# Second layer of a two-layer graph network: LayerNorm's gain folded into the weights, and a group's scattered products summed in one PSUM bank before they are added

## The reference

```
h = concat(x[src], x[dst], edge_attr) @ W1 + b1                  # one row per edge
h = relu((h - mean(h)) * rsqrt(var(h) + 1e-5) * ln_g + ln_b)     # LayerNorm with gain and bias
messages = (h @ W2 + b2) * sigmoid(edge_attr @ gate_w + gate_b)
agg = segment_sum(messages, dst)                                 # sum of an edge's row into its node
gi, gh = agg @ W_ih.T + b_ih, x @ W_hh.T + b_hh                  # then a GRU step per node
x = layernorm(x + gru(gi, gh, x))
```

## Time and profile before

| what | us |
|---|---|
| device time, three runs | 5134.09, 5176.93, 5184.84 |
| median of these | 5176.93 |
| span of the profiled execution, first to last instruction | 5142.6 |
| of it: sort and schedule | to about 472 |
| first layer | to about 2640 |
| second layer | to 5142.6 |

### The profile page before, as it was taken

One profiled execution on the slowest core, in us unless ns is written; L12 is line 12 of the kernel. 1 busy time (PEld: TensorE's weight loads), 2 busy tenths in 40 slices (PEclk: granted clock), 3 DMA queues, 4 the chain that ended last, 5 costly groups with the idle time before them and its releaser, 6 DMA issues. The chain is left out here.

```text
span 5142.6 us, 108062 instructions
## 1 busy us (share of the span) xinstructions
PE 3506.5 (68%) x20734; PEld 3121.8 (61%) x20735; DVE 4015.9 (78%) x15806; ACT 2380.6 (46%) x6569; POOL 3316.3 (64%) x3375
## 2 busy tenths in 40 slices
PE   5543666666666666666547877777777777777776
PEld 4432555656665565655547767666666666666665
DVE  8995677777777777777758988877877877877876
ACT  2211233333333333333336665665665655665654
POOL 0004777777777777777747777666666666666661
PEclk9655677776767777678868898888889888898887
DMA  3113445555555554555444444333333333333331
GB/s 105 45 35 92 130 139 145 145 142 145 145 142 144 146 145 142 143 144 145 142 107 106 108 110 105 97 96 98 94 96 100 96 92 100 95 95 100 98 94 40
DMA packets 597657, 576.83 MB, mean 112 GB/s; under 512 B 320530, under 2 KB 462744, under 8 KB 597312
## 3 DMA queue, kind: packets, MB, share of 16 engines
q0 software_dynamic: 133952, 329.07, 23.6%
q1 hardware_dynamic: 463360, 244.62, 17.8%
HBM read 536.53 MB, written 43.09 MB: 113 GB/s over the span
## 5 line engine op out<-in xcount | busy, mean ns | idle before, releaser
L1662 POOL DMA_INDIRECT crows<-c,gather_index x1664 | 1666.9, 1002 | 738.8 <-issue 469.7
L1187 POOL DMA_INDIRECT bxrows<-bx,gather_index x1664 | 1620.0, 974 | 507.5 <-issue 506.0
L1222 PE MATMUL scattered<-bxrows,hotw 128*128 128x129 f32 x3328 | 695.2, 378 | 552.7 <-DVE hotw L1385 552.0
L1222 PEld LDWEIGHTS scattered<-bxrows,hotw 128*128 128x128 f32 x3328 | 604.7, 272 | 634.5 <-DVE acc L1382 553.9
L1710 PE MATMUL scattered<-z,hotw 128*128 128x129 f32 x3328 | 560.1, 336 | 503.3 <-DVE hotw L1912 503.2
L1710 PEld LDWEIGHTS scattered<-z,hotw 128*128 128x128 f32 x3328 | 518.3, 242 | 534.8 <-issue 489.5
L1891 DVE SCALAR_TENSOR_TENSOR z<-h,rstd,ln_g 128x128 f32<-128x128 f32 x1664 | 577.6, 347 | 237.8 <-issue 237.5
L1212 PE MATMUL pre<-near,hotT 128*128 x3328 | 595.1, 352 | 211.2 <-DVE h L1360 177.8
L1695 PE MATMUL pre<-w1e,efT 128*128 128x129 f32 x3328 | 691.6, 291 | 66.8 <-DVE h L1883 34.0
L1382 DVE TENSOR_TENSOR acc<-acc,scattered 128x129 f32 x1664 | 471.2, 283 | 326.2 <-ACT mask L1293 320.6
L1212 PEld LDWEIGHTS pre<-near,hotT 128*128 128x128 f32 x3328 | 558.1, 260 | 261.2 <-issue 257.9
(11 more groups left out here) (268 smaller groups left out, 5599.5 us busy)
## 6 DMA issues: line engine op xcount, KB each, us to landing
spread<-place_rows SPq DMA_DIRECT2D x416, 256.0 KB, 3.5
ef<-in_edge_attr SPq DMA_DIRECT2D x1664, 32.0 KB
bxrows<-bx,gather_index POOLq DMA_INDIRECT x1664
crows<-c,gather_index POOLq DMA_INDIRECT x1664
x_turned<-x1T SPq DMA_DIRECT2D x98, 64.0 KB
g_xT<-x_turned SPq DMA_DIRECT2D x98, 64.0 KB
x_a<-in_x SPq DMA_DIRECT2D x97, 64.0 KB
x_b<-in_x SPq DMA_DIRECT2D x97, 64.0 KB
```

The costliest lines, as they stand in the source:

```text
L1187: pool.indirect_dma_start(out=bx[q][:, k, 0:2 * D], out_offset=None, in_=s.bx[:, :], in_offset=bass.IndirectOffsetOnAxis(ap=s.index[:, g * ...
L1222: last = nc.tensor.matmul(out[:, k // 2, k % 2, 0:W], hotw[v % 2][:, k, :], bx[v][:, k, D:D + W], start=True, stop=True)
L1662: pool.indirect_dma_start(out=crows[q][:, k, 0:D], out_offset=None, in_=s.c[:, :], in_offset=bass.IndirectOffsetOnAxis(ap=s.index[:, g * G ...
```

## The change

1. **ln_g is folded into the weights.** `centre` multiplies W1's columns with the sign of ln_g, `copy_folded` multiplies the rows of the folded GRU weights with its size (at least 1e-30). Since relu(a·size + b) = size·max(a, -b/size) + b, line 1891 can now take the maximum with -ln_b/size (`floor_b`) itself, as its second operation, in place of the multiplication with ln_g. The separate maximum (line 1907, two instructions a group) and its semaphore `scaled` go. Four small dependent instructions at the head of the second layer make `floor_b`.
2. **From group 37 on (`FIRST_JOINED`) a group's products are summed on PE.** The sorting by rounds leaves a group of eight steps with at most three different tiles from there on. PE clears three places of one bank with a matmul of zeros (`nothing`), and then lets all eight products accumulate, each at the place of its tile: the tile of step 0 at place 0, the tile of step 7 at place 2, any other at place 1. The place is a register value, from a new table `spot_of`, which `schedule_stage` makes and PE loads as eight registers for each group. DVE adds three sums in place of eight products, after all eight z rather than between them. Groups 0 to 36 still add eight.
3. **Loops.** `joined_slots` stands in the place of `loop_slots`: rounds 4 to 9 are written out, the loop with node work has rounds 10 to 51, and its bodies are of the joined kind. POOL's program is as before.

```diff
         for j in range(2):
-            dve.tensor_scalar(s.w1cd[:, j * D:(j + 1) * D], raw[:, j, :], mean[:, j:j + 1], None, ALU.subtract)
+            dve.scalar_tensor_tensor(s.w1cd[:, j * D:(j + 1) * D], raw[:, j, :], mean[:, j:j + 1], sign_g[:, :],
+                                     ALU.subtract, ALU.mult)
...
-        dve.tensor_copy(fold[:, :], m_ps[:, :, :].rearrange("p j d -> p (j d)")).then_inc(rows_done, 1)
+        dve.tensor_scalar(fold[:, :], m_ps[:, :, :].rearrange("p j d -> p (j d)"), size_g[:, 0:1], None,
+                          ALU.mult).then_inc(rows_done, 1)
...
+                        dve.tensor_copy(tile_rows[own, :], tile_turned).then_inc(spotted, 1)
...
+                        dve.scalar_tensor_tensor(spot_i[own, :], same_last[own, :], 1.0, same_first[own, :],
+                                                 ALU.add, ALU.mult).then_inc(spotted, 1)
...
+JOINED = 10
+FIRST_JOINED = JOINED * R - 3
+LEADS = (0, 3, 7)
+def joined_slots(engine, steps, nodes, last):
+    def body(o):
+        for q in range(R):
+            steps(o * R + q, q, o, o >= JOINED)
+            nodes(o * R + q, q, o)
+    body(0)
+    with engine.Fori(1, 4) as o:
+        for q in range(R):
+            steps(o * R + q, q, o, False)
+    for o in range(4, JOINED):
+        body(o)
+    with engine.Fori(JOINED, BODIES) as o:
+        for q in range(R):
+            steps(o * R + q, q, o, True)
+            nodes(o * R + q, q, o)
...
+def sums_added(n):
+    if isinstance(n, int) and n <= FIRST_JOINED:
+        return n * G + 1
+    return n * 3 + (FIRST_JOINED * (G - 3) + 1)
...
+                sp.dma_start(spot_of, s.spot_of[:, :]).then_inc(steps_in, 16)
...
-                    if has(g, 3):
+                    if has(g, 3) and joined:
+                        par = (q - 3) % 2
+                        spots = load_values(nc, mybir.EngineType.PE, spot_of[0:1, bass.ds((g - 3) * G, G)], 2 * W)
+                        pe.wait_ge(added, sums_added(g - 3))
+                        nc.tensor.matmul(out[:, 0, 0:3 * W], nothing[:, 0:P], nothing[:, :], start=True, stop=False)
+                        for k in range(G):
+                            if k % 4 == 0:
+                                pe.wait_ge(hotw_made, g * 2 - 5 + k // 4)
+                                pe.wait_ge(z_made, g * 2 - 5 + k // 4)
+                            last = nc.tensor.matmul(out[:, 0, bass.ds(spots[k], W)], hotw[par][:, k, :],
+                                                    z[par][:, k, :], start=False, stop=(k == G - 1))
+                        last.then_inc(scattered, 1)
+                    elif has(g, 3):
...
-                                                            rstd[:, par, k:k + 1], ln_g[:, :], ALU.mult, ALU.mult)
+                                                            rstd[:, par, k:k + 1], floor_b[:, :], ALU.mult, ALU.max)
                             if k % 4 == 3:
-                                last.then_inc(scaled, 1)
-                        if has(g, 3):
+                                last.then_inc(z_made, 1)
+                        if has(g, 3) and not joined:
...
-                        if has(g, 2) and k % 4 == 3:
-                            half = k // 4
-                            dve.wait_ge(scaled, g * 2 + half - 3)
-                            part = z[par][:, 4 * half:4 * half + 4, 0:D]
-                            dve.tensor_tensor(part, part, spread_b, ALU.max).then_inc(z_made, 1)
+                    if has(g, 3) and joined:
+                        dve.wait_ge(scattered, g + (FIRST_JOINED * 2 - 2))
+                        for j, k in enumerate(LEADS):
+                            dve.wait_ge(added, sums_added(g - 3) + j)
+                            place = acc[:, bass.ds(tiles[k], 1), 0:W]
+                            dve.tensor_tensor(place, place, out[:, 0:1, j * W:(j + 1) * W], ALU.add).then_inc(added, 1)
```

More of the change, by code:

```diff
@@ L751, in schedule_stage @@
         side_rows = one("side_rows", [P, BLOCKS, P], I32)
-        edge_i, chunk_x = one("edge_i", [BLOCKS, P], I16), one("chunk_x", [P, BLOCKS], F32)
+        edge_i, chunk_x = one("edge_i", [BLOCKS, P], I16), one("chunk_x", [P, 32 + BLOCKS], F32)
+        own = slice(32, 32 + BLOCKS)
+        tile_rows, same_first, same_last, spot_i = (
+            one(n, [32 + BLOCKS, P], t) for n, t in (("tile_rows", F32), ("same_first", F32), ("same_last", F32),
+                                                     ("spot_i", I16)))
         tile_sq, ones_sq = one("tile_sq", [P, P], BF16), one("ones_sq", [TILES, TILES], F32)
@@ L787, in _ @@
                 sp.dma_start(s.edge_of.rearrange("a (b p) -> (a b) p", p=P), edge_i[:, :]).then_inc(stored[1], 16)
+                sp.wait_ge(spotted, 4)
+                sp.dma_start(s.spot_of.rearrange("a (b p) -> (a b) p", p=P), spot_i[own, :]).then_inc(stored[1], 16)
                 for l in LAYERS:
@@ L936, in _ @@
                     if l == 1:
-                        dve.tensor_tensor(chunk_x[:, :], chunk_f[l][:, :], by_block[l][:, :, 2],
-                                          ALU.add).then_inc(chunk_copied, 1)
+                        dve.tensor_tensor(chunk_x[:, 0:BLOCKS], chunk_f[l][:, :], by_block[l][:, :, 2], ALU.add)
+                        dve.tensor_copy(chunk_x[:, own], by_block[l][:, :, 0]).then_inc(chunk_copied, 1)
                 for l in LAYERS:
@@ L1478 @@
 BEHIND = 4
+JOINED = 10
+FIRST_JOINED = JOINED * R - 3
+LEADS = (0, 3, 7)
+assert FIRST_JOINED * G // TILES >= 3
+def joined_slots(engine, steps, nodes, last):
[13 more added lines that the diff above has]
+            nodes(o * R + q, q, o)
+    for g in range(GROUPS, last + 1):
+        steps(g, g % R, g // R, True)
+        nodes(g, g % R, g // R)
+def sums_added(n):
+    if isinstance(n, int) and n <= FIRST_JOINED:
+        return n * G + 1
+    return n * 3 + (FIRST_JOINED * (G - 3) + 1)
 THIRDS = [(0, 3), (3, 6), (6, G)]
@@ L1489, in layer1_stage @@
         sem = s.sem
-        step_rows = sb("step_rows1", [2, STEPS], I16)
-        tile_of, edge_of = step_rows[0:1, :], step_rows[1:2, :]
+        step_rows = sb("step_rows1", [3, STEPS], I16)
+        tile_of, edge_of, spot_of = step_rows[0:1, :], step_rows[1:2, :], step_rows[2:3, :]
+        nothing = sb("nothing", [1, 3 * W], BF16)
         spread = [sb(f"spread1_{q}", [P, G * P], BF16) for q in range(2)]
@@ L1673, in _, with steps @@
                 pe.wait_ge(aug_ready, 1)
-                def steps(g, q, o):
+                def steps(g, q, o, joined):
                     if has(g, 0):
@@ L1746, in nodes @@
                         last.then_inc(n_made, 1)
-                loop_slots(pe, steps, nodes, LAST)
+                joined_slots(pe, steps, nodes, LAST)
             @block.scalar
@@ L1857, in _ @@
                 dve.memset(eps[:, :], 1e-5)
+                dve.memset(nothing[:, :], 0.0)
                 dve.memset(augT[:, :], 1.0).then_inc(aug_ready, 1)
@@ L2001, in program @@
         s.tile_order = [nc.dram_tensor(f"tile_order{l}", (1, TILES), I16).ap() for l in range(2)]
-        s.edge_of = nc.dram_tensor("edge_of", (1, STEPS), I16).ap()
+        s.edge_of, s.spot_of = (nc.dram_tensor(n, (1, STEPS), I16).ap() for n in ("edge_of", "spot_of"))
         s.index1, s.place1 = (nc.dram_tensor(n, (P, STEPS), t).ap() for n, t in (("index1", I32), ("place1", F32)))
```

98 lines of the change are left out of this document (64 added, 34 removed).

## The result

The changed kernel takes 4856.88 us (median of 4 runs, 4849.13 to 4887.46) against 5178.77 us (4 runs, 5134.09 to 5184.84): a ratio of **0.943, 95% interval 0.937 to 0.949**. The profiled execution has a span of 4854.2 us and a time of 4857.32; the span of before was 5142.6, so the trace to be explained is 288.4 us shorter. The prediction had said 279 for that difference and 4898 us for the median.

A forecast was written before the change was run, and what follows sets the result against it. The prediction took DVE to bound the kernel after group 36. -276 us for 171 groups, +1 at the start and -4 at the end gave -279, from 5176.9 to 4898 us; whole range 4845 to 4975.

The forecast's parts named there:

- POOL becomes the bound: Second layer after group 36: POOL's 32 gathers a round, 41.4 us, outlast DVE's round of 36.9 us; forecast chance 0.73.
- The top of a round, 4.5 us: DVE's issue idle time before first h and z, 3.60 and 2.45 us, loses 4.5 us a round; other bound 0.
- z and adds, 1.55 us a slot: DVE from first z to first hotw: 4.94 us falls to 3.4, saving 1.55 a slot, 6.2 a round.
- DVE's round of 36.9 us: DVE's loop round: 47.57 less 6.2 for z and adds and 4.5 at the top; 41.4 if the top stays.
- the rival in which DVE stays the bound: Top keeps its 4.5 us and adds cost their upper bound: 43.8 us a round, 4998 us; chance 0.17.
- The sum, -276 for 171 groups: Groups 36 to 207 at 8 gathers of 1.295 us take 1771.6 us instead of 2047.9, h following POOL at 12.2 us.
- PE's second load at nothing, zeros 0.4 to 0.7 us: PE's added register load, 1.93 us a slot, hidden; zeros matmul 0.4 to 0.7 us; PE's round 38.3, below 41.4.
- the two PE rivals: PE's register loads exposed: new one alone 46.0 us a round, 5096 us, chance 0.06; both 53.7, 5425 us, 0.03.
- The wait for the whole group, covered by 1.3 us: DVE's first add waits for all eight products; 5.8 us of DVE work ahead covers at most 3.80 + 0.7.
- Groups 0 to 36 at nothing, the start at +1: Groups 0 to 36 lose their maxima but POOL sets their pace: nothing; small extra instructions in `centre` cost about 1 us.
- The end, -4 us: After h of group 207, 62.0 us: cheaper z and adds and fewer last adds save 4 us (0 to 5.5).
- The median, 4898: Whole-kernel time: median 5176.9, 34 us above the profiled span, less 279; own range 4874 to 4925.

The follow-up runs named there:

- half of the gathers: Every second gather of layer 2 left out, part of the sums missing: changed kernel 4599.59 us, ratio 0.893; kernel before 5150.46 us, ratio 0.999.
- both shift runs: The kernel before with 64 or 256 one-column memsets on DVE ahead of layer 2's loops, loop untouched: ratios 0.960 and 1.002.
- the folding alone: The changed kernel with folded weights but no group joined, eight adds one by one, no zeros, no second register load: 4850.36 us, ratio 0.943.
- the joining alone: The changed kernel with joined products but ln_g not folded, so two maxima a slot return on DVE: 4890.22 us, ratio 0.952.
- the kernel moved by 64: The kernel before with 64 memsets on DVE ahead of layer 2's loops, so its loop starts 64 instructions later: 4934.95 us, ratio 0.960.
- the one moved by 256: Control: the kernel before with 256 memsets on DVE ahead of layer 2's loops: 5154.34 us, ratio 1.002.
- the 16 matmuls: 16 extra matmuls on PE, results overwritten, ahead of the first layer's products: changed kernel 4847.07 us, folding alone 4841.94 us, kernel before 5140.51 us.
- the folding with half of the gathers: The folding alone with every second gather of layer 2 left out, part of the sums missing: 4715.87 us.
- the gate on ACT: The changed kernel with the gate computed on ACT by logarithm and exponential instead of DVE's add and reciprocal: 4892.49 us, ratio 0.945.

## Why the prediction was right, step by step

- **POOL becomes the bound:** shown. With half of the gathers the 171 groups of the changed kernel gain 210 us and those of the kernel before 9.
- **The top of a round, 4.5 us:** right in size (2.45 us went to 1.01; ahead of the first h DVE now waits for gathers, and with half of them out the 3.60 are 0.28), and for the reason given: where the loop lies decides, as both shift runs show. The count that the prediction leaned on, 217 instructions being fewer than the 262 that don't stall, isn't what decides: 273 don't stall in the folding alone, and 289 don't when they lie 64 places further on. By the Trainium skill's rule ("Runtime: NRT & Kernel Launch", instruction fetch mechanics) the other bound, 0, was never live for this body, since 217 instructions can't touch three blocks of 256.
- **z and adds, 1.55 us a slot:** measured 1.77 (4.94 to 3.17). The folding brings the larger part: in the folding alone the phase of the last group takes 3.78 us (z at 4790.33, hotw at 4794.11 in its trace). The joining is worth 1.9 us a round once POOL is out of the way. With POOL as the bound neither size of the joining's share is seen in the time; without the joining the kernel is as fast.
- **DVE's round of 36.9 us:** at most 36.2, the round with POOL out of the way, so the rival in which DVE stays the bound (41.4 to 43.8) falls.
- **The sum, -276 for 171 groups:** measured -287.9. The term that was off is the gather's pitch: from the first gather of group 36 (3019.02 us) to that of group 207 (4776.65) it is 1.285 us instead of 1.295, inside the bounds of 1.280 and 1.310. The other term, h at 12.2 us behind its group's first gather, is 11.3 at group 36 and 13.7 at group 207, which gives 2.4 us back. The prediction had feared that gathers get longer when all engines work more densely; they got shorter, 981 ns instead of 1002 in the mean. The maxima aren't the cause, since the joining alone has them and 981 ns too; the kernel moved by 64 has 986, the one moved by 256 has 1005. What it is in the stalled loop that lengthens them stays open.
- **PE's second load at nothing, zeros 0.4 to 0.7 us:** the zeros take 0.33 to 0.53 us, 0.33 as a rule. The load of places is hidden even at a round of 36.2 us, and that round lies below the 46.0 and 53.7 of the two PE rivals, so both fall. The prediction's reason, that a load runs while the engine works off what was issued, holds for this load and not for the load of tile numbers: with half of the gathers out that one leaves PE idle for some 2 us a round. While POOL sets the pace this isn't seen in the time.
- **The wait for the whole group, covered by 1.3 us:** right in the loop, where the adds of the round above start without a gap. At the end, where DVE has neither h nor z of a next group ahead of the add, it isn't covered: the last group's adds wait 2.15 us for PE's products.
- **Groups 0 to 36 at nothing, the start at +1:** -2.3 us up to h of group 36. The reason, that POOL sets the pace there, was right by a margin of 5 us only (half of the gathers left out of the kernel before).
- **The end, -4 us:** off by 6 us in the profiled execution, where the span after the last h grew by 1.9, and right in another, of the same code (below). The saving came: the last group's adds end 21.0 us behind the last h (4811.3) instead of 26.3 (5106.8). PE's node products behind them gave it back. First PE's timeline of before there, then the same products after:

```profile
5102.98 0.70 PE L1731 MATMUL bank_gru<-wfold_sb,g_T 128*128 128x256 f32 x2 [0.82 <-ACT augT L1822]
5103.52 0.59 PE L1732 MATMUL bank_gru<-whh_sb,g_xT 128*128 128x256 f32 x2
```

```profile
4811.68 1.22 PE L1812 MATMUL bank_gru<-wfold_sb,g_T 128*128 128x256 f32 x2 [0.82 <-ACT augT L1903]
4812.69 1.06 PE L1813 MATMUL bank_gru<-whh_sb,g_xT 128*128 128x256 f32 x2
```

  And the granted clock (the number behind the five busy times), before from 5103 to 5108 us and after from 4811 to 4819:

```profile
5103.00:5108.00 5.00, 3.42 (x12) 1.92 (x12) 2.92 (x10) 1.44 (x2) 0.00 (x0) 1.00 0.07 18
```

```profile
4811.00:4819.00 8.00, 6.38 (x12) 3.35 (x12) 0.88 (x3) 1.44 (x3) 0.00 (x0) 0.50 0.06 16
```

  Before, PE had 2.4 GHz for these twelve matmuls, after it had 1.2 GHz, as it had from 4796 us on. But this comes and goes in the changed kernel. With the 16 matmuls ahead of the first layer its end is the same code; there the granted clock is 0.99 from 4804 to 4811 us, and the same products are as short as before:

```profile
4806.00 0.70 PE L1819 MATMUL bank_gru<-wfold_sb,g_T 128*128 128x256 f32 x2 [0.82 <-ACT augT L1910]
4806.54 0.59 PE L1820 MATMUL bank_gru<-whh_sb,g_xT 128*128 128x256 f32 x2
```

  58.0 us follow its last h, 4.1 less than the 62.0 of the kernel before, which is what was forecast. Of the five traces of the changed kernel and its variants with joined groups and folded weights, three have 63.3 to 63.9 us after the last h and two 58.0 and 58.2; the five of the kernel before and its variants all have 61.8 to 62.1. The folding alone has a granted clock of 0.97 from 4806 to 4812 us and needs 59.2. Some 13 to 16 us ahead of these products PE had waited in all three kernels: 4.75 us for DVE's hotw in the kernel before, 3.85 us for DVE's adds in the changed kernel, and 5.88 us with the 16 matmuls. What decides whether the clock comes back is open.
- **The median, 4898:** 41 us too high, and the forecast's own range (4874 to 4925) missed it; the whole range held. The sum was taken off a median that lay 34 us above the profiled span, and the median after lies 3 us above its span. The step that failed is the assumption that this offset belongs to the kernel and stays: it comes and goes from one execution to the next.

## What to carry to other kernels

An "issue" gap of some us at a loop's top that another loop with the same work lacks is worth one cheap test before anything is rewritten: move the loop by a few dozen instructions, and by a whole block as a control. When an edit makes the next engine the bound, half of that engine's work left out tells what the edit's parts are worth, which the time itself no longer does. When an added instruction changes nothing, count it in the trace first: it may not be there. And a median should be set against the profiled span by the stage that differs, not carried over as an offset.

## What had not been expected of the hardware

The 36 us between runs sit in one place: PE's products ahead of the first layer. The busy times of that stretch in the changed kernel, and in the changed kernel with the gate on ACT, where the stretch is the same code (PE's count first, granted clock behind the five):

```profile
50.00:96.00 46.00, 45.97 (x279) 36.39 (x278) 37.55 (x46) 18.39 (x60) 0.00 (x0) 1.00 0.52 146
```

```profile
50.00:132.00 82.00, 81.97 (x279) 64.50 (x278) 38.20 (x48) 18.76 (x60) 0.00 (x0) 1.00 0.30 84
```

The same 279 matmuls take 46 us in one execution and 82 in the other, one pair 0.48 us or 0.79, while the granted clock stands at 1.00 beside both. The first h of the whole kernel starts at 494.6 us in one and at 529.9 in the other. Of the first ten traces, those of the kernel moved by 256, of the folding with half of the gathers and of the gate on ACT have the long one, the other seven the short one. By its times the kernel before has it in 29 of its 62 runs, those above 5160 us; the others lie at 5131 to 5149. With PE busy in the 18 us ahead of it, none of the 12 runs of the two changed kernels lay 36 us high, but three of the 12 of the kernel before did. So the idle time ahead isn't shown to be what decides, and the cause is open.
